# The last steps of a local-attention kernel in an order of their own, with the last norm as a stage of them

## The reference, cut to what matters

```python
for i in range(DEPTH):                                  # DEPTH = 6
    x = attn_layer(shift_tokens(x), Wqkv[i], ...) + x   # 16 heads of 64, windows of 32 keys and the 32 before
    x = ffn_layer(shift_tokens(x), ...) + x             # norm, W1 to 2*341 columns, a * gelu(gate), W2
...
x = _layernorm(x + _L0_attn_ref(x, ...))
x = _layernorm(x + _L0_ffn_ref(x, ...))                 # the six layers are _L0_ffn_ref
```

## Time and profile before

| | |
|---|---|
| median of 3 runs | 1984.67 us (1978.17 to 1985.89) |
| profiled execution: its time | 1989.52 us |
| profiled execution: its span, first to last instruction | 1987.7 us |
| mean granted clock of TensorE, share of full speed | 0.966 |
| busy: TensorE / weight loads | 1803.6 us (91%) / 998.0 us (50%) |
| busy: VectorE / ScalarE / GpSimd | 1534.6 (77%) / 1366.4 (69%) / 1266.6 us (64%) |
| last step with a quarter's projections begins on TensorE | about 1869 us |
| last addition of the last unit ends | 1963.9 us |
| last norm, from ScalarE's first copy to the end | 1964.2 to 1987.7 us |

### The profile page before, as it was taken

The page is one execution under the profiler, slowest core; times in us unless marked ns, Lnnn a source line. Parts: engine busy times, 40 slices in busy tenths (PEclk is TensorE's granted clock), DMA queues, the critical chain, the costliest instruction groups (busy, mean ns, idle before and its releaser), DMA issues. The chain is left out here.

```text
span 1987.7 us, 59622 instructions
## 1 busy us (share of the span) xinstructions
PE 1803.6 (91%) x24192; PEld 998.0 (50%) x24192; DVE 1534.6 (77%) x2549; ACT 1366.4 (69%) x2874; POOL 1266.6 (64%) x1127
## 2 busy tenths in 40 slices
PE   5898889668899999999999999999999999999974
PEld 3443444345455555555555555555555555555541
DVE  4778787347788888888888888888888888888833
ACT  1454444447787777887778877788777887778832
POOL 4303210238877877878778787787877778778710
PEclk8899999889999999999999999999999999999986
DMA  9000000323433334333343333433334333233300
GB/s 184 15 2 1 2 2 2 85 51 71 92 83 81 74 71 92 83 81 73 75 88 86 79 73 71 92 84 81 73 75 89 82 83 71 66 70 83 79 1 22
DMA packets 137216, 132.63 MB, mean 67 GB/s; under 512 B 79336, under 2 KB 82984, under 8 KB 136616
## 3 DMA queue, kind: packets, MB, share of 16 engines
q1 hardware_dynamic: 136944, 128.81, 29.2%
HBM read 20.94 MB, written 1.05 MB: 11 GB/s over the span
## 5 line engine op out<-in xcount | busy, mean ns | idle before, releaser
L1023 ACT ACTIVATE prob<-s_in,lower,rq 128x64 f32<-128x64 f32 x1536 | 535.2, 431 | 1.8 <-POOL lower L1191 1.6
L827 PE MATMUL bank_a<-x_shift,wqk_sb 128*128 128x512 f32 x768 | 368.0, 602 | 6.0 <-ACT sq L1136 4.2
L1009 ACT ACTIVATE zT<-bank_z 128x1024 f32<-128x1024 f32 x192 | 193.0, 1017 | 86.3 <-PE bank_z L838 86.3
L1162 POOL TENSOR_TENSOR prob<-prob,rden 128x1024 f32<-128x1024 f32 x96 | 182.9, 1905 | 96.8 <-DVE rden L1242 96.7
L827 PEld LDWEIGHTS bank_a<-x_shift,wqk_sb 128*128 128x128 f32 x768 | 146.3, 194 | 185.2 <-issue 178.1
L1181 POOL TENSOR_TENSOR kfin<-rk,kfin 128x512 f32<-128x512 f32 x96 | 122.4, 1275 | 174.4 <-ACT rk L1117 116.6
L384 ACT ACTIVATE a_prob<-a_sT 128x1024 f32<-128x1024 f32 x128 | 130.6, 1024 | 105.5 <-PE a_sT L218 103.4
L493 DVE TENSOR_REDUCE a_negmax<-a_max 128x1 f32<-128x512 f32 x256 | 164.7, 685 | 48.0 <-PE a_max L168 44.2
L846 PE MATMUL bank_y<-zT,wvo_high 128*128 128x512 f32 x384 | 187.9, 612 | 0.9 <-ACT zT L1009 0.9
L846 PE MATMUL bank_y<-zT,wvo_low 128*128 128x512 f32 x384 | 187.2, 610 | 0.6 <-ACT zT L1009 0.4
L838 PE MATMUL bank_z<-pT,xk_prev 32*128 32x128 f32 x3072 | 166.2, 285 | 16.5 <-DVE xn L1275 12.1
(11 more groups left out here) (176 smaller groups left out, 4009.8 us busy)
## 6 DMA issues: line engine op xcount, KB each, us to landing
kpad<-kfin SPq DMA_DIRECT2D x384, 128.0 KB, 2.4
qpair<-qfin SPq DMA_DIRECT2D x384, 128.0 KB, 2.4
wqk_sb<-in_wqkv SPq DMA_DIRECT2D x40, 128.0 KB, 2.7
xk_prev<-xk_own SPq DMA_DIRECT2D x24, 192.0 KB, 2.4
ffn_sb<-in_ffn SPq DMA_DIRECT2D x6, 537.5 KB, 4.3
wvo_low<-in_wqkv SPq DMA_DIRECT2D x6, 256.0 KB, 5.6
wvo_low<-in_wo SPq DMA_DIRECT2D x3, 512.0 KB, 6.7
wvo_high<-in_wqkv SPq DMA_DIRECT2D x6, 256.0 KB, 5.1
```

The costliest lines, as they stand in the source:

```text
L827: last = pe.matmul(bank_a[:, half, :], wqk_sb[:, layer_of(u) % 2, part, half, g * P:(g + 1) * P], cols(u), start=True, stop=True)
L1009: return act.activation(out, in_, ACT.Copy)
L1023: last = act.activation(prob[:, n % 2, i, :], s_in[:, n % 2, i, :], ACT.Exp, bias=lower[:, n % 2, i:i + 1], scale=rq[:, n % 2, i:i + 1])
L1162: pool.tensor_tensor(prob[:, e % 2], prob[:, e % 2], rden[:].unsqueeze(2).broadcast_to([P, TPB * GH, 2 * WIN]), ALU.mult).then_inc(pn_ok, 1)
```

## The change

Steps 0 to 95 keep their order on every engine. `STEPS_ALL` was 105 and is 107. From step 96 on (`s >= QUARTERS`) four things differ:

- VectorE takes the maximum of quarter 95 right behind its mask, and sums, divides and transposes the quarter whose exponentials ScalarE makes in the same step (d instead of e).
- ScalarE makes 16 exponentials in one piece, makes both copies of the weighted rows one behind the other, and loads Gelu's table once, behind the exponentials of quarter 95.
- Unit 23 turns its tiles in `bank_y` instead of banks 2 and 3 of `bank_z`, and its linear half of W1 goes to `bank_a` and `bank_y`, so that TensorE does not wait for `gelu_ok`; VectorE does.
- The last norm of sequences 0, 1, 2 and 3 is a stage at steps 97, 102, 103 and 105 (`LAST`). TensorE turns each half of the channels by itself straight from `x_shift`, eight pieces, into banks that are free; VectorE adds them in two halves into `pk` and normalizes into `pq` in the next step. `last_norm` and ScalarE's copies for it are gone.

```diff
@@ -46,7 +46,8 @@
 QUARTERS = UNITS * GROUPS
 LAG_FF = 7
 ADD, SUM, NORM, GATE, LINEAR, OUTPUT = 0, 1, 2, 3, 4, 5
-STEPS_ALL = QUARTERS+4+OUTPUT
+LAST = {QUARTERS + 1: UNITS - 4, QUARTERS + 6: UNITS - 3, QUARTERS + 7: UNITS - 2, QUARTERS + 9: UNITS - 1}
+STEPS_ALL = QUARTERS + 11
...
+        def turned_half(half, b):
+
+            bank = bank_z if b else bank_a
+            return bank[:, half, (b % 2) * 2 * P:(b % 2 + 1) * 2 * P].rearrange("p (t n) -> p t n", n=64)
+
+        def turn_bank(u, own):
+
+            return bank_y[:] if u == UNITS - 1 else bank_z[:, own, :]
+
+        def linear_banks(u):
+
+            return (bank_a[:, 0, :], bank_a[:, 1, :], bank_y[:]) if u == UNITS - 1 else (bank_z[:, 2, :], bank_z[:, 3, :], bank_f[:])
...
@@ -818,6 +842,11 @@
             sp.wait_ge(kpad_zero, 1)
             for s in range(STEPS_ALL):
                 step(s)
+                if s - 1 in LAST:
+                    b = LAST[s - 1] % B
+                    sp.wait_ge(y_f, b + 1)
+                    sp.dma_start(out_v[b], tokens(pq, b)).then_inc(stored, 16)
+            sp.wait_ge(stored, 16 * B)
...
                 for stage, back, ok in ((NORM, 0, xn_ok), (NORM, 1, xnT_ok), (GATE, LINEAR - GATE, gelu_ok), (LINEAR, 1, hid_ok),
                                         (OUTPUT, 1, xf_ok)):
                     v = unit_at(s - back, stage)
-                    if v is not None:
+                    if v is not None and (stage != GATE or s < QUARTERS):
                         after(pe, ok, v)
...
                 if u_lin is not None:
-                    after(pe, gelu_ok, u_lin)
-                    first_half(bank_z[:, 2, :], u_lin, 0, 0)
-                    first_half(bank_z[:, 3, :], u_lin, 0, 1)
+                    if u_lin < UNITS - 1:
+                        after(pe, gelu_ok, u_lin)
+                    for j, bank in enumerate(linear_banks(u_lin)[0:2]):
+                        first_half(bank, u_lin, 0, j)
                     after(pe, floor_ok, min(n, QUARTERS - 1))
                     after(pe, floorq_ok, min(c, QUARTERS - 1))
-                    first_half(bank_f, u_lin, 0, 2).then_inc(lin_mm, 1)
+                    first_half(linear_banks(u_lin)[2], u_lin, 0, 2).then_inc(lin_mm, 1)
...
+                if s in LAST:
+                    u, b = LAST[s], LAST[s] % B
+                    pe.wait_ge(sqq_ok, QUARTERS)
+                    pe.wait_ge(pq_ok, QUARTERS)
+                    pe.wait_ge(xf_ok, u + 1)
+                    if b:
+                        pe.wait_ge(z01_ok, QUARTERS)
+                        pe.wait_ge(total_f, b)
+                    for t in range(TPB):
+                        for half in range(2):
+                            rows, at = slice(64 * half, 64 * half + 64), b * XW + t * P + half
+                            last = pe.matmul(turned_half(half, b)[:, t, :], x_shift[rows, at:at + P], ident[rows, rows],
+                                             start=True, stop=True, is_transpose=True, skip_group_check=True)
+                    last.then_inc(turn_f, 1)
...
+                if s >= QUARTERS:
+                    if u_gelu is not None:
+                        after(act, gate_mm, u_gelu)
+                        after(act, ff_mm, u_gelu - 1)
+                        for j, bank in ((2, bank_f), (0, bank_z[:, 2, :]), (1, bank_z[:, 3, :])):
+                            m = min(P, FF - j * P)
+                            last = act.activation(hid[0:m, j, :], bank[0:m, :], ACT.Gelu, bias=ff_column(u_gelu, FCH + j)[0:m])
+                        last.then_inc(gelu_ok, 1)
+                    if quarter(d):
+                        after(act, lower_ok, d)
+                        after(act, pT_ok, d - 2)
+                        after(act, den_ok, d - 2)
+                        exponentials(d, 0, 16).then_inc(exp_ok, 1)
+                    if d == QUARTERS - 1:
+                        act.preload_act_table(ACT.Gelu)
+                    u_turned = unit_at(c, NORM)
+                    if u_turned is not None:
...
+                        act.activation(xnT[:], turn_bank(u_turned, 3), ACT.Identity, bias=ff_column(u_turned, 2 * FCH + 2), scale=ff_column(u_turned, 2 * FCH + 1)).then_inc(xnT_ok, 1)
+                    if quarter(c):
+                        after(act, floorq_ok, c)
+                        after(act, lower_ok, c - 2)
+                        act.activation(rq[:, c % 2], rq_sum[:], ACT.Ln).then_inc(lnq_ok, 1)
+                        after(act, lnq_ok, c)
+                        act.activation(rq[:, c % 2], rq[:, c % 2], ACT.Exp, bias=log8[:], scale=-0.5).then_inc(rq_ok, 1)
+                    if quarter(e):
+                        after(act, z_mm, e)
+                        after(act, y_mm, e - 2)
+                        z = zT[:, e % 2].rearrange("p w t h q -> p w (t h q)")
+                        copy(z[:, 2:4, :], bank_z[:, 2:4, :]).then_inc(z23_ok, 1)
+                        copy(z[:, 0:2, :], bank_z[:, 0:2, :]).then_inc(z01_ok, 1)
+                elif u_gelu is not None:
...
+                if s - 1 in LAST:
+                    b = LAST[s - 1] % B
+                    pool.wait_ge(mv_f, b + 1)
+                    if b:
+                        pool.wait_ge(y_f, b)
+                    pool.tensor_tensor(f_rstd[:], f_mv[:, :, 1], eps[:, 0:TPB], ALU.add).then_inc(eps_f, 1)
+                    pool.wait_ge(eps_f, b + 1)
+                    pool.tensor_tensor(f_rstd[:], f_rstd[:], halfneg[:, 0:TPB], ALU.pow).then_inc(rstd_f, 1)
...
-                if quarter(e):
+                if s - 1 in LAST:
+                    b = LAST[s - 1] % B
+                    dve.wait_ge(rstd_f, b + 1)
+                    for t in range(TPB):
+                        last = dve.tensor_scalar(pq[:, b, t * P:(t + 1) * P], pk[:, b, t * P:(t + 1) * P], f_mv[:, t, 0:1],
+                                                 f_rstd[:, t:t + 1], ALU.subtract, ALU.mult)
+                    last.then_inc(y_f, 1)
+                if quarter(e) and s <= QUARTERS:
...
-                if quarter(e):
+                if quarter(e) and s <= QUARTERS:
...
+                if quarter(c) and s >= QUARTERS:
+                    after(dve, mask_ok, c)
+                    after(dve, lower_ok, c - 1)
+                    dve.tensor_reduce(s_max[:], s_in[:, c % 2], AX.X, ALU.max, negate=True).then_inc(max_ok, 1)
+                if quarter(d) and s >= QUARTERS:
+                    after(dve, exp_ok, d)
+                    dve.tensor_reduce(den[:], prob[:, d % 2], AX.X, ALU.add).then_inc(den_ok, 1)
+                    after(dve, den_ok, d)
+                    after(dve, pn_ok, d - 1)
+                    dve.reciprocal(rden[:], den[:]).then_inc(rden_ok, 1)
+                    after(dve, pn_ok, d)
+                    after(dve, z_mm, d - 2)
+                    dve.transpose(pT[:, d % 2].rearrange("p k h q -> p h k q"),
+                                  prob[:, d % 2].rearrange("p h (k n) -> p h k n", n=WIN)).then_inc(pT_ok, 1)
...
-                if quarter(c):
+                if quarter(c) and s < QUARTERS:
...
                     after(dve, lin_mm, u_lin)
-                    for j, bank in enumerate((bank_z[:, 2, :], bank_z[:, 3, :], bank_f)):
+                    if u_lin == UNITS - 1:
+                        dve.wait_ge(gelu_ok, UNITS)
+                    for j, bank in enumerate(linear_banks(u_lin)):
...
+                if s in LAST:
+                    b = LAST[s] % B
+                    dve.wait_ge(turn_f, b + 1)
+                    dve.wait_ge(rotk_ok, QUARTERS)
+                    dve.wait_ge(qfin_ok, QUARTERS)
+                    for half in range(2):
+                        part = slice(64 * half, 64 * half + 64)
+                        last = dve.tensor_tensor(tokens(pk, b)[:, :, part], turned_half(half, b),
+                                                 x1_tok[:, b * TPB:(b + 1) * TPB, part], ALU.add)
+                    last.then_inc(total_f, 1)
+                    dve.wait_ge(total_f, b + 1)
+                    for t in range(TPB):
+                        last = dve.bn_stats(f_stats[:, t, :], pk[:, b, t * P:(t + 1) * P])
+                    last.then_inc(stats_f, 1)
+                    dve.wait_ge(stats_f, b + 1)
+                    if b:
+                        dve.wait_ge(y_f, b)
+                    for t in range(TPB):
+                        last = dve.bn_aggr(f_mv[:, t, :], f_stats[:, t, :])
+                    last.then_inc(mv_f, 1)
```

99 lines of the change are left out of this document (19 added, 80 removed).

## The result

The changed kernel takes 1964.45 us in the median of four runs (1951.7 to 1965.49), the kernel before 1984.99; the ratio is 0.9883, 95% interval 0.9859 to 0.9906, so 18.7 to 28.0 us less (the quotient of the two medians alone would be 0.9897). Beside the experiments further down it ran again: 1957.06 us against 1985.9, ratio 0.9856 (0.9840 to 0.9873). The first profiled execution has a span of 1963.7 us and a time of 1965.49.

What follows compares the result with a forecast made beforehand. The prediction took the end, from step 96, as a chain of waits with no engine full. Gains 8.5 + 0.3 - 0.1 + 15.1 = 23.8 us, so 1984.7 - 23.8 = 1961 us; range 1954 to 1970.

Steps and rivals of the forecast that it cites:

- the likeliest case: The outcome given most weight: a time of 1957.5 to 1964.5 us, chance 0.53.
- the signs: Right if: maximum before 1893.5, quarters 94 and 95 on time, unit 23's products waiting for VectorE, under 9 us behind last addition.
- One sign of being wrong: The first 1889 us, ahead of the changed steps, differing by more than 2 us would show the forecast wrong.
- Quarter 94: On TensorE it begins at about 1903.9 instead of 1908.64, 4.7 us earlier, ScalarE's first copy at 1896.23 not moving.
- Quarter 95: On TensorE, starts at 1911.2 instead of 1919.75, 8.5 us earlier, with the new turns of batch 0 priced at 0.9 us.
- The rival of the low clock: The stretch 1903.9 to 1911.2 runs low: 1963.5 us, or 1970 if low up to unit 22's gate; chance 0.16.
- Banks: Unit 23's linear half no longer waits for the gate's activation; products begin 8.8 us earlier, 0.3 from this edit.
- Behind the products: From unit 23's products to its last addition, the norm of batch 2 on VectorE costs 0.1 us; addition ends 1955.2.
- The last norm: Behind unit 23's last addition only batch 3 is left: 8.7 us instead of 23.8, a gain of 15.1.
- Table loads: Three of ScalarE's four switches behind 1900 go, costed at nothing; 8.0 us by the skill if none were covered.
- the end of the gate: From quarter 95 to unit 23's gate, order and waits stay; 8.5 us carried through, ending 1940.6 instead of 1949.1.
- the turned piece: Eight pieces of 64 rows replace four tiles in the norm's turns on TensorE: 1.45 us at low clock, 0.9 high.

Runs made afterwards that it cites:

- experiment 10: The changed kernel itself, unaltered, run again beside the variants on one chip: 1957.06 us, ratio 0.9856 to the kernel before.
- experiment 8: The kernel of experiment 6 plus products of constants that nobody reads in four idle times of TensorE: 1953.42 us, ratio 0.9839.
- Experiments 1 to 3: The changed kernel with the old order behind step 96 on VectorE and ScalarE, on ScalarE alone, on VectorE alone: 1968.74, 1973.91 and 1970.12 us.
- experiment 4: The changed kernel with unit 23 back in its old banks, its linear half waiting for the gate's Gelu: 1959.49 us, ratio 0.9864.
- experiments 4 and 11: experiment 4, and the kernel before with only the last norm as stages, the first at step 98, old order and banks: 1966.84 us, ratio 0.9909.
- experiment 6: The changed kernel with the norm of sequence 1 one step earlier, 101 instead of 102: 1955.61 us, ratio 0.9845.
- experiment 9: The kernel of experiment 8 with VectorE's normalization of sequence 2 moved behind unit 23's last addition: 1948.95 us, ratio 0.9819.

## Why the prediction was right

The forecast was 1961 us; the two medians are 1964.5 and 1957.1, the ratios mean 23.2 and 28.6 us against 23.8. By the first trace, 24.35 us from the mask, less the 0.35 by which the mask was later. The first median lies just inside the likeliest case (1957.5 to 1964.5), the second just below it. Of the signs, three came as said (the maximum at 1893.16, unit 23's products behind the normalization of sequence 1, 8.2 us behind the last addition); quarters 94 and 95, at 1905.41 and 1912.38, came later than the 1903.5 to 1904.5 and 1911 to 1912 that I had named. One sign of being wrong was of no use: with the same code the last mask of the repeat (experiment 10) ends 5.5 us earlier than in the first trace, so a change of over 2 us in the first 1889 us says nothing. Point by point:

- *Quarter 94.* Predicted 11.1 us behind the mask (1903.9 less 1892.77), measured 12.29, and 11.15 to 11.7 in the six other profiles with this order and no filling. The step that was off is the sentence that ScalarE's first copy "does not move": it came at 1897.28, since quarter 93's weighted rows ran wholly at the low clock this time (0.91 for a group at 1893.34). TensorE had idled 3.38 us in front of them in both kernels; in the kernel before, the clock fell only in the middle of these rows. In experiment 8, where 0.76 us of that idle time is left, it stayed high and quarter 94 started at 9.98. The mechanism, normalization of unit 22 as what ends last, is in the row at 1905.41.
- *Quarter 95.* Predicted 7.3 us behind quarter 94, measured 6.97: the turned pieces took 0.39 us (1909.21 to the next product at 1909.60) and not 0.9. Experiments 1 to 3 show that it needed both queues. My walk had the two edits one after the other and so could not say that each is worth little alone.
- *The rival of the low clock* did not come where it was put: from quarter 94 to quarter 95 the granted clock is 1.00. The clock was low at quarter 93, for 1.2 us that the forecast did not have.
- *Banks.* Worth 0.3 us by my sum; by experiment 4 nothing in front of the products, and a cost of 1.2 us behind them. The 1.6 us by which the stretch from the gate to the products shrank come with the stages of the last norm, old banks or new (experiments 4 and 11). That the norm of sequence 1 would be what the products wait for was right: its normalization ends where they begin (1945.25 and 1946.28 in the rows), and experiment 6, which moves it, frees 2.3 us. From the gate to the products I had 6.3 us, measured 4.91: the turns in front of that norm were priced 1.06 too high, the rest is the norm itself (4.6 for 4.7) and the gate's last product.
- *Behind the products.* I had a cost of 0.1 us; it was 0.94. The term took W2 at its old price, and W2 ran low throughout, 5.5 us instead of 4.55; TensorE had idled 3.59 us in front of it, in the kernel before 2.25, since the new banks let it end the linear half earlier. When it runs high, the norm of sequence 2 holds the addition at 6.5 us (experiments 4, 6 and 8). So the stages between cost something either way, which experiment 9 gives back.
- *The last norm.* 15.1 predicted, 15.57 measured; most of the difference is the turns, 0.86 us from the last addition to VectorE's sum instead of 1.45.
- *Table loads* were worth nothing that a row shows. ScalarE's wait in front of the Gelu of unit 23 grew from 3.88 us to 4.81 where a load was taken away. The estimate of 8.0 us, from the 2.66 us a switch by the Trainium skill (ScalarE: Activation LUTs, "What ACT_TABLE_LOAD costs"), would have needed a ScalarE without such waits. The drain that the page counts in those 2.66 us does not show in this trace: a load of the changed kernel that starts at 1622.61 lasts 1.28 us, and the Gelu behind it starts at 1623.90.

From the mask to the end I had 71.1 us, measured 70.6. Too low were quarter 94 by 1.2 and W2 by 0.9; too high the stretch to quarter 95 by 0.3, that to the end of the gate by 0.4, that from the gate to the products by 1.4 and the last norm by 0.5. They cancel, so the agreement of the sum is partly luck; the term that was mis-sized everywhere is the turned piece: eight took 0.39 us at the high clock where I had 0.9, and loads of 0.53 us at the low one (experiment 10) where I had 1.45. What stays open is why the first 96 steps scatter by 9 us from one execution to the next; the granted clock over the span differs with it (the kernel of experiment 9 took 1956.78 us at 0.973 and 1946.5 at 0.980), but nothing here tells cause from effect.

## What to carry to other kernels

Where a software pipeline runs out of work, the order that served its full steps is a queue of waits: walk the last steps with the durations of the trace, and put into each idle time what is ready. Two engines that feed each other must be reordered together; either alone gave 1.2 to 1.5 us of 7.7, in one execution each. A stage moved off the end stands in somebody's queue, so ask at each place what waits behind it: the norm of sequence 1 one step earlier and the normalization of sequence 2 behind the last addition, with TensorE kept busy, were worth another 0.4% on the same chip. And a wait taken from TensorE can come back as idle time further on, and cost more there by the clock than it gave: here the new banks cost 1.2 us.
